# Expert blocks in two parts, woven into the end of the attention stage, in a cross-attention and mixture-of-experts kernel

## The reference, cut to what matters

```python
q_prime, k_prime = relu(qh) + EPS_K, (relu(kh) + EPS_K) * em       # linear cross-attention
kv = jnp.einsum('bhnd,bhne->bhde', k_prime, vh)
...
att = jax.nn.softmax(jnp.where(causal, q @ k.T / sqrt(hd), -inf))  # self-attention, per head
...
logits = flat @ gate_W + gate_b
top_v, top_i = jax.lax.top_k(logits, TOP_K)                        # TOP_K = 2
w = jax.nn.softmax(top_v, axis=-1)
for e in range(NUM_EXPERTS):                                       # 8
    mid = jax.nn.gelu(flat @ exp_W1[e] + exp_b1[e], approximate=False)
    out = out + w_full[:, e:e + 1] * (mid @ exp_W2[e] + exp_b2[e])
```

## Time and profile before

| | us |
|---|---|
| median of 3 runs (576.87 to 579.16) | 579.07 |
| the profiled execution | 577.21 |
| its span, first to last instruction | 575.4 |
| TensorE busy | 492.3 (86%) |
| VectorE busy | 400.5 (70%) |
| POOL busy | 326.4 (57%) |
| ScalarE busy | 284.0 (49%) |

### The profile page before, as it was taken

How to read it: one execution, slowest core, us unless ns; L and a number is a source line. 1 busy time by engine, 2 the same in 40 slices (tenths; PEclk the granted TensorE clock), 3 DMA queues, 4 the chain that set the end, 5 groups by cost and what they waited for, 6 DMA issues and landing times.

```text
span 575.4 us, 13859 instructions
## 1 busy us (share of the span) xinstructions
PE 492.3 (86%) x4469; PEld 405.7 (71%) x4469; DVE 400.5 (70%) x1239; ACT 284.0 (49%) x686; POOL 326.4 (57%) x349
## 2 busy tenths in 40 slices
PE   2998899999998999999999998942299999999920
PEld 2655578778777777777767866732299999999920
DVE  5775878999899899799799786425055555555536
ACT  2215338467466565565566555311166555656510
POOL 4625546557778778678768667345245545454520
PEclk9999899999999999999999999655599999999975
DMA  4920100100200200100000000001467777767639
GB/s 95 223 71 0 39 2 1 38 2 2 58 19 3 56 21 14 44 20 1 21 19 11 21 9 25 16 19 52 140 197 203 200 215 209 205 197 217 190 115 327
DMA packets 57851, 47.71 MB, mean 83 GB/s; under 512 B 15406, under 2 KB 44465, under 8 KB 57780
## 3 DMA queue, kind: packets, MB, share of 16 engines
q1 hardware_dynamic: 53460, 38.35, 24.5%
q0 software_dynamic: 4320, 8.47, 4.3%
HBM read 35.18 MB, written 12.08 MB: 82 GB/s over the span
## 4 chain that ended last, share of the span: by engine, by line
PE 45%; DVE 26%; issue 9%; POOL 8%; DVEq 4%; DMA 3%; ACT 2%; SPq 1%; POOLq 0%
PE bank L721 11%; PE bank L731 11%; POOL sorted_rows L1125 3%; PE bank L456 3%; PE bank L536 3%; DVE mx L1415 2%; DVE places L1383 2%; PE bank L563 2%; PE bank L541 2%; PE bank L373 2%; DVE places L1292 2%; POOL rs L989 2%; DVE vbd L1404 1%; PE bank L713 1%; DVE places L1288 1%
## 5 line engine op out<-in xcount | busy, mean ns | idle before, releaser
L1184 POOL DMA_INDIRECT result_rows<-back,rows x71 | 69.6, 980 | 77.1 <-DVE back L1641 74.9
L964 ACT ACTIVATE mid<-bank,b 128x128 f32<-128x128 f32 x284 | 81.2, 369 | 52.5 <-PE bank L721 52.5
L1125 POOL DMA_INDIRECT sorted_rows<-send,slot_u x64 | 64.1, 1002 | 29.2 <-issue 14.4
L1107 POOL TENSOR_TENSOR km<-kb,head 128x512 f32<-128x512 f32 x56 | 58.2, 1044 | 34.0 <-ACT kb L834 22.3
L721 PE MATMUL bank<-hT,w 128*128 128x128 f32 x568 | 76.7, 279 | 0.1
L731 PE MATMUL bank<-w,mid 128*128 x568 | 74.9, 275 | 0.0
L563 PEld LDWEIGHTS bank<-vbd,pT 128*128 128x128 f32 x512 | 65.4, 197 | 13.3 <-ACT pT L859 5.9
L721 PEld LDWEIGHTS bank<-hT,w 128*128 128x128 f32 x568 | 70.4, 195 | 0.6 <-issue 0.5
L563 PE MATMUL bank<-vbd,pT 128*128 128x36 f32 x512 | 66.6, 277 | 4.6 <-DVE places L1427 2.8
L731 PEld LDWEIGHTS bank<-w,mid 128*128 128x128 f32 x568 | 68.9, 192 | 0.0
L536 PE MATMUL bank<-km,qbd 128*128 128x512 f32 x128 | 67.8, 612 | 0.0
(11 more groups left out here) (204 smaller groups left out, 983.2 us busy)
## 6 DMA issues: line engine op xcount, KB each, us to landing
w<-in_L_ffn_exp_W_dram SPq DMA_DIRECT2D x79, 256.0 KB, 3.6
rows<-sorted_rows SPq DMA_DIRECT2D x71, 65.0 KB
places<-result_rows SPq DMA_DIRECT2D x16, 256.0 KB
places<-in_x_dram SPq DMA_DIRECT2D x8, 256.0 KB, 2.9
places<-in_ctx_dram SPq DMA_DIRECT2D x8, 256.0 KB, 3.4
out_dram<-acc SPq DMA_DIRECT2D x8, 256.0 KB, 5.8
result_rows<-back,rows POOLq DMA_INDIRECT x71, 3.0
sorted_rows<-send,slot_u POOLq DMA_INDIRECT x64, 2.4
```

The lines of the kernel that those rows point to most:

```text
L964: A(mid[s][:, c, :], hidden[2 * s + c // 2][:, c % 2 * P:c % 2 * P + P], ACT.Gelu, bias=b1[:, bass.ds(expert, 1), c]).then_inc(mid_ok, 1)
L1107: G.tensor_tensor(km[n % 2][:, :, :], kb[u][:, n % 2, t * S:t * S + S].unsqueeze(1).broadcast_to([P, HG, S]), head8[:, :].unsqueeze(2).bro ...
L1125: G.indirect_dma_start(out=sorted_dram, out_offset=bass.IndirectOffsetOnAxis(ap=slot_u[u][:, j // 2, t:t + 1], axis=0), in_=send[u][:, t, ...
L1184: G.indirect_dma_start(out=result_dram, out_offset=bass.IndirectOffsetOnAxis(ap=rows[s][:, D:D + 1].bitcast(U32), axis=0), in_=back[s % 4] ...
```

## The change

The last beats (10 to 12) are written out call by call on each engine. The 71 blocks fall into two parts: the first 41 (`SURE`) are whole blocks of 128 rows that the first six groups (`FIRST`) fill in any case, and have a table of their own, computed between the score units of the last group; the other 30 come from a second table, computed between blocks 11 and 27. Groups 6 and 7 are called `PREV` and `LAST`. The steps that route group 7 (and the end of group 6's) stand between blocks, one step per block on each engine. `gates` no longer needs the exponential: the two weights are 0.5 -/+ 0.5 tanh(gap / 2), written by `weights`. The Gelu table is loaded once ahead of the first block (`ahead`). ScalarE's queue issues twelve loads of results (groups 0 to 5) between blocks 60 and 70 and all eight stores; SP loads only groups 6 and 7. The transposed rows of a block have one bank in place of two. At the start, group 1's inputs are loaded before 16 of the 18 smaller weights.

```diff
+    FIRST = 6
+    SURE = -((E * (P - 1) - 2 * FIRST * N) // P)
+    WHOLE = (2 * FIRST * N + E * (P - 1)) // P
+    PART_BLOCKS = (SURE, BLOCKS - SURE)
+    RESULTS_AT = WHOLE + 5
...
-                for dst, src in other_weights:
+                for dst, src in other_weights[0:2]:
                     sp.dma_start(dst, src).then_inc(w_loaded, 16)
                 load(1, 1)
+                for dst, src in other_weights[2:]:
+                    sp.dma_start(dst, src).then_inc(w_loaded, 16)
...
+                def wait_part(p):
+                    for u in LANES:
+                        sp.wait_ge(scattered[u], (FIRST, GROUPS)[p] // 2 * 2 * T * 16)
+                    if p == 1:
+                        sp.wait_ge(blanked, E * 16)
+                    sp.wait_ge(table_ok, p + 1)
...
+                    if i == PART_BLOCKS[0]:
+                        wait_part(1)
...
+                    load_block(i, experts[i - at], places_of[i - at])
+                    if 0 <= i - (PART_BLOCKS[0] - E - 3) < E:
+                        blank_tail(i - (PART_BLOCKS[0] - E - 3))
...
+                rows_T(0)
+                rows_T(1)
+                middle(0)
+                blocks(0, 1)
+                ranks(PREV)
+                pe.wait_ge(y_ok, GROUPS * T)
+                blocks(1, 3)
+                y_T(LAST)
+                blocks(3, 5)
+                project_out(LAST)
+                blocks(5, 13)
+                a_T(LAST)
+                blocks(13, 15)
+                gate_logits(LAST)
+                blocks(15, 18)
+                ranks(LAST)
+                blocks(18, 21)
+                count_rows(1)
+                blocks(21, BLOCKS)
...
-                    A(dlt[:, :], dlt[:, :], ACT.Exp).then_inc(e_ok, 1)
+                    A(dlt[:, :], dlt[:, :], ACT.Tanh, scale=0.5).then_inc(e_ok, 1)
...
+                a_normal(PREV, (0, 1))
+                a_normal(PREV, (2, 3))
+                copy_pT(LAST, 5)
+                exp_scores(LAST, 6)
+                copy_pT(LAST, 6)
+                exp_scores(LAST, 7)
+                copy_h2T(PREV)
+                A(ahead[:, :], ahead[:, :], ACT.Gelu)
+                copy_pT(LAST, 7)
...
+                for s in range(RING):
+                    act.wait_ge(returned[s], ((WHOLE - s) // RING + 1) * 16)
+                load_results(0, 0)
+                for n in range(1, 2 * FIRST):
+                    load_results(n // 2, n % 2)
+                    if RESULTS_AT + n - 1 < BLOCKS:
+                        blocks(RESULTS_AT + n - 1, RESULTS_AT + n)
+                for g in ALL:
+                    store(g)
...
+                        if i >= BLOCKS - 3:
+                            add_results(i - BLOCKS + 3)
...
+                blocks(0, 3)
+                weights(PREV)
+                slots(PREV)
+                blocks(3, 6)
+                add_residual(LAST)
+                blocks(6, 7)
+                a_stats(LAST)
+                blocks(7, 8)
+                a_variances(LAST)
+                blocks(8, 10)
+                a_offset(LAST)
+                blocks(10, 12)
+                begun_blocks(0)
+                blocks(12, 13)
+                segments()
+                blocks(13, 16)
+                copy_logits(LAST)
+                top_two(LAST)
+                gates(LAST)
+                blocks(16, 19)
+                weights(LAST)
+                slots(LAST)
+                blocks(19, 22)
+                take_counts(1)
+                tails()
+                blocks(22, 23)
+                begun_blocks(1)
+                blocks(23, 24)
+                second_lengths()
+                blocks(24, 25)
+                pass_ends(BLOCKS - SURE, 2 * E)
+                blocks(25, 26)
+                count_passed(BLOCKS - SURE, 2 * E)
+                blocks(26, 27)
+                second_table()
+                blocks(27, BLOCKS)
```

649 lines of the change are left out of this document (458 added, 191 removed).

## The result

The changed kernel takes **566.12 us** (median of 4 runs, 563.27 to 568.41) beside 579.12 for the kernel before (4 runs, 576.87 to 581.71): ratio 0.973, 95% interval 0.968 to 0.979. It is faster, as forecast, but by 13 us where 35 were forecast, and 566 lies outside the range of 533 to 558.

A forecast was written before the change was run, and what follows sets the result against it. TensorE bounds attention and blocks, with a latency chain between them and another at the end. Span 575.4 - 37.5 + 8.2 + 3.3 + 1.0 - 9 = 541.4, plus 1.8 around it and 1.9 to the median: 544 us, range 533 to 558.

The forecast's parts named there:

- `middle(0)` earlier: Start of the blocks: the first block product at 376.2 in place of 413.7, 37.5 us earlier, bounds 33 and 41.
- steps among the blocks: VectorE's steps put behind `weigh` at 15 places, each free up to about 0.5 us: 8.2 us, between nothing and 16.6.
- TensorE's steps: Extra TensorE work among the blocks (`y_T`, `project_out`, `a_T`, `gate_logits`, two `ranks` and the count): 3.3 us.
- POOL's lag: Blocks 3 to 11: returns and scatters put POOL 4.3 us behind, 3.3 us of slack; cost 1.0 us, between 0 and 4.
- the end: Last `weigh` to the end: most result loads and adds leave the chain, 15.1 us for 23.9; -9, between -6 and -11.
- the likeliest case: The forecast as worked out, 544 us, own range 536 to 552; chance 0.62.
- The walk: Last group's attention in the new order: unit 2 at 347.4, unit 7 at 362.9, then a chain to `middle(0)` at 376.2.
- five times 2.6 and 2.5 us: Units 2 to 7: five rounds of 2.6 us, plus 2.5 us for VectorE's first table and group 6's statistics.
- `a_offset` of group 6 (0.5 us): First item of the chain from unit 7 to `middle(0)`, taken at 0.5 us; 2.24 beside POOL's `keep_residual` was a bound.
- VectorE becomes the bound among the blocks: Rival: steps cost full length, POOL's lag its bound (8.4 + 3 us), the clock falls at some: 555 us; chance 0.17.
- The end collides: Rival: result loads delay weights (+6) and final chain (+3), or SP's blanking delays loads: 554 to 560 us; chance 0.08.
- Slower: Rival: stalls among the blocks drop TensorE to 1.2 GHz and keep it there; 590 us with 30 such blocks; chance 0.03.

The follow-up runs named there:

- kind A: Comparison groups in which the kernel before took 579 to 582 us; the changed kernel's ratio to it was 0.973 and 0.968.
- Pool later: Changed kernel with GpSimd's keep_residual(6) and z_bias(7) moved from ahead of the blocks to behind its blocks 1 and 2; 565.47 us, ratio to the kernel before 0.974.
- apart: Changed kernel with VectorE's steps ahead of blocks 8, 16 and 24, where registers are loaded, moved one block off; 562.25 us, ratio to the kernel before 0.967.
- aligned: Changed kernel with the second table moved seven columns, so pieces begin at multiples of eight; 557.38 us (0.961 to the kernel before), in B 593.11 (0.995).
- together: Changed kernel with table columns moved seven, VectorE steps off register-load blocks, GpSimd's two additions held until e_off is written; 552.14 us (0.947), in B 581.17 to 588.24.
- results last: Changed kernel with the old end: SyncE loads all results after the last scatter, all additions behind the blocks; 600.95 us in B, ratio to the kernel before 1.012.
- B: Comparison groups in which the kernel before took 594 to 597 us; the changed kernel's ratio to it was 1.002, 0.997 and 1.000.

## Why the prediction was wrong

In the step's own terms, for the profiled execution of kind A (forecast, then measured, us of span):

| term | forecast | measured |
|---|---|---|
| `middle(0)` earlier | -37.5 | -29.1 |
| steps among the blocks, TensorE's steps, POOL's lag | +8.2 +3.3 +1.0 | +15.4 (blocks 0 to 39) |
| blocks 40 to 70 | 0 | +7.9 |
| the end | -9 | -7.9 |
| sum | -34.0 | -13.7 |

**What bounds the kernel** was read rightly: the hole of the earlier trace rows went, TensorE became the bound of all that was left, and the order of the likeliest case (faster, gain from the start and the end, part given back in the blocks) came.

**The start: 8.4 us short.** The walk had unit 2 at 347.4, unit 7 at 362.9 and `middle(0)` at 376.2; the trace has 348.98, 368.18 and 384.69. 1.6 us were late ahead of unit 2, 1.4 of them already at unit 1, whose scores I had set at 342.17 "in both" and which start at 343.60. The step "five times 2.6 and 2.5 us" was 3.7 short: in the five rounds stand also `y_T` and `project_out` of group 6 (0.44 and 0.89 us to the next instruction in this trace), which I had left out, two waits of 1.20 and 0.92 for `attended`, and a stretch of 3.4 us at half clock. The chain from there, "`a_offset` of group 6 (0.5 us)" and on, was 3.2 short, 2.7 of it the 3.23 us of `e_off`. The earlier trace rows showed 2.24 us beside GpSimd's work, and I had it as a bound and took the lower value. The row held more than I read in it, for that `e_off` too ended (356.79) with a second GpSimd instruction, behind `keep_residual` of 354.50:

```profile
355.73 1.03 POOL L1107 TENSOR_TENSOR km<-kb,head 128x512 f32<-128x512 f32 x1
```

In the diff two additions of 1.28 and 1.27 us follow one another, and the price is both. "Pool later" and the pair of rows under it confirm it. The items of my chain add up to 10.0 us, where its result needs 10.8; that slip brings the forecast nearer to the measured time. The table load cost no more than its row: it began 0.02 us behind the copy ahead of it and its Gelu came 0.01 us behind it, so the 1.4 us that the Trainium skill's page (ScalarE: Activation LUTs, What ACT_TABLE_LOAD costs) would add did not show, and all of it lay beside TensorE's transposes and value products.

**Blocks 0 to 39: 15.4 where 12.5 were forecast.** Of this 9.6 us are TensorE's waits by the list, 6.8 of them for `turn`. Its places were the named ones, the largest after block 15 (2.40 us, with 1.5 forecast). Two things offset one another: some 0.65 us were free at each place, not 0.5, but three places carried a register load as well (0.6 to 0.8 us, which I had costed nowhere; "apart" gave 2.9 us back), and one carried a `weigh` of 1.63 us beside GpSimd's `keep_residual(7)` (414.19). TensorE's own steps took some 3.8 us from start to next start, near the forecast 3.3; the rest, some 2 us, is spread over blocks that took 2.0 us in place of 1.90 behind a wait. The full price of VectorE's steps, my bound, adds up to 16.2 us and not 16.6. POOL's lag cost nothing: VectorE hardly ever waited for a return.

**Blocks 40 to 70: 7.9 where nothing was forecast.** This is the step that failed outright. I had never priced a register load, though the trace of before has them and my own list of VectorE's order behind block 15 shows one. 5 us are the start columns ("aligned", 67.3 to 62.3 us). Some 2 us are the twelve result loads, behind block 60. The last microsecond no run explains.

**The end: right.** 14.9 us from the last `weigh`, with 15.1 forecast; it starts 1.1 us later against TensorE's end. For the loads' crowding I took 0 and kept up to 6, though my own sum of the share (1.2) left no room for 0; it is 1 to 2. So the rule of the Trainium skill (DMA: Bandwidth & Descriptors, Issuing engines are not separate DMA queues), that another queue brings no bandwidth, agrees in kind with the windows of `together` and `results last`.

**The rivals.** "VectorE becomes the bound among the blocks" (555) was nearest in time but not in cause: VectorE's share was 9.6 us against 8.2. "The end collides" had a quarter of its price; "Slower" did not come in A. In B a part of its mechanism came, half clock behind stalls among the blocks, for 10 to 29 us but not for good, and the kernel was as fast as the one before. The range was too narrow because every bound was taken from steps that I had listed; three costs (register loads, a second GpSimd addition beside a small VectorE step, two TensorE steps in the rounds) were in no term. That the whole gain depends on the occasion (13 and 18 us in A, none in B) was in no rival either.

## What to carry to other kernels

When a serial stage is moved into one whose engines are all busy, price everything that stands between the moved steps too: register loads, their start columns, and instructions of GpSimd that run beside short VectorE steps. Where such a step is on the critical path, let GpSimd wait for it. A table that engines read in pieces of eight should begin each piece at a multiple of eight; seven unused entries cost nothing that could be seen. And a schedule that fills the idle half microsecond of each block may have lost the cushion that hid late work (argued here, not shown): judge it on several occasions, not one.

## What the runs showed of the hardware

- A register load of eight entries took 0.5 to 0.9 us, in most blocks up to 0.66, when it began at a multiple of eight, and 1.7 to 2.0 us (in B up to 2.2) when it did not, on SyncE, ScalarE, TensorE and VectorE alike.
- Three VectorE instructions that work in SBUF alone (128x4, 1x256 and 128x128) lasted until GpSimd's additions beside them had ended, and at most 0.3 us longer: 0.16 became 3.23 us, 0.43 became 2.07, 0.29 became 1.56 and 1.63. Not all do: `weigh` kept its 0.29 beside GpSimd's small `e_rs` (128x4, at 410.40). Score maxima, which read PSUM, kept their 0.69 us.
- The same two kernels stood at 579 and 566 us in one comparison and at 596 and 596 in another, once on one chip. Why is open.
